# A wait between groups of gathers, and another order of the steps of tile 1

## The reference, cut to what matters

```python
def _L0_rec_ref(dense_features, sparse_features):
    combined = jnp.concatenate([dense_features[:, None, :], sparse_features], axis=1)
    interactions = jnp.einsum('bfd,bgd->bfg', combined, combined)
    iu, ju = jnp.triu_indices(FEATURE_NUM, k=1)
    return interactions[:, iu, ju]
e = jnp.stack([tbl_0[ids[:, 0]], ..., tbl_25[ids[:, 25]]], axis=1)
z = _L0_rec_ref(r_dense_features, e)
h = jnp.concatenate([z, r_dense_features], axis=1)
h = jnp.maximum(h @ W_top1 + b_top1, 0.0)
h = jnp.maximum(h @ W_top2 + b_top2, 0.0)
y = h @ W_top3
```

## Time and profile before

| | us |
|---|---|
| time, median of 3 runs | 511.42 (511.13 to 512.32) |
| the profiled execution's own time | 512.17 |
| its span, first to last instruction | 510.4 |
| TensorE busy | 360.0 (71%) |
| GpSimd busy | 254.2 (50%), 256 gathers |
| VectorE busy | 242.9 (48%) |
| ScalarE busy | 153.6 (30%) |
| mean granted clock of TensorE | 0.839 of full speed |

### The profile page before, as it was taken

One profiled execution on the slowest core, in us unless ns is written; L12 is line 12 of the kernel. 1 busy time (PEld: TensorE's weight loads), 2 busy tenths in 40 slices (PEclk: granted clock), 3 DMA queues, 4 the chain that ended last, 5 costly groups with the idle time before them and its releaser, 6 DMA issues.

```text
span 510.4 us, 13987 instructions
## 1 busy us (share of the span) xinstructions
PE 360.0 (71%) x6224; PEld 332.2 (65%) x6224; DVE 242.9 (48%) x172; ACT 153.6 (30%) x269; POOL 254.2 (50%) x260
## 2 busy tenths in 40 slices
PE   7695516977279763989369782897459882798927
PEld 6583406966179762989259781896439881797826
DVE  4995703827048270745429370673509451380220
ACT  2462401234122331324132241233232341223512
POOL 5887560655506474265635755264734745165000
PEclk9988656999569995899759986898959986698978
DMA  7992230211202131121303112131312112111000
GB/s 198 251 278 54 55 90 7 79 43 51 78 17 80 36 87 46 34 65 39 94 26 77 46 45 79 29 74 31 102 31 66 47 41 84 26 54 41 16 15 1
DMA packets 23322, 33.32 MB, mean 65 GB/s; under 512 B 6565, under 2 KB 15397, under 8 KB 23303
## 3 DMA queue, kind: packets, MB, share of 16 engines
q0 software_dynamic: 8192, 16.79, 12.6%
q1 hardware_dynamic: 14926, 16.20, 11.8%
q10 hardware_dynamic: 186, 0.09, 0.1%
HBM read 29.97 MB, written 0.01 MB: 59 GB/s over the span
## 4 chain that ended last, share of the span: by engine, by line
PE 56%; issue 18%; another core or an unknown queue 14%; ACT 7%; DMA 3%; SPq 2%; DVE 1%; ACTq 0%; DVEq 0%
PE psum L458 31%; PE psum L483 11%; PE psum L472 3%; DMA lows<-table 3%; ACT feats L336 3%; PE psum L548 3%; PE psum L496 2%; PE psum L497 2%; PE psum L498 2%; ACT gram L336 2%; PE psum L540 1%; ACT h L378 1%; SPq L208 1%; ACT dense_hi L336 1%
## 5 line engine op out<-in xcount | busy, mean ns | idle before, releaser
L252 POOL DMA_INDIRECT rows<-table,idx x256 | 254.0, 992 | 215.0 <-PE psum L472 114.2
L277 DVE TENSOR_TENSOR onehot<-ids_b,psum 125x2048 fp32r<-125x2048 int16 x80 | 180.2, 2283 | 18.5 <-PE psum L458 12.3
L260 DVE COPY gram<-psum 26x416 f32<-26x416 f32 x64 | 37.4, 584 | 182.6 <-PE psum L483 181.1
L336 ACT ACTIVATE feats<-psum 128x512 f32<-128x512 f32 (+1 forms) x120 | 77.4, 689 | 148.1 <-PE psum L458 106.9
L458 PE MATMUL psum<-onehot,hot_hi 125*128 125x256 f32 x640 | 99.2, 299 | 11.1 <-issue 6.8
L483 PE MATMUL psum<-feats 128*26 128x26 f32 x4096 | 64.3, 211 | 59.6 <-issue 55.7
L483 PEld LDWEIGHTS psum<-feats 128*26 128x26 f32 x4096 | 55.9, 125 | 70.8 <-issue 64.8
L458 PE MATMUL psum<-onehot,hot_lo 125*128 125x256 f32 x640 | 95.6, 291 | 4.4 <-issue 4.3
L458 PEld LDWEIGHTS psum<-onehot,hot_hi 125*128 125x128 f32 x640 | 86.5, 200 | 14.2 <-issue 9.0
L458 PEld LDWEIGHTS psum<-onehot,hot_lo 125*128 125x128 f32 x640 | 86.7, 198 | 6.3 <-issue 5.6
L336 ACT ACTIVATE gram<-psum 26x416 f32<-26x416 f32 (+1 forms) x72 | 35.5, 494 | 73.1 <-PE psum L483 54.5
(11 more groups left out here) (26 smaller groups left out, 167.7 us busy)
## 6 DMA issues: line engine op xcount, KB each, us to landing
lows<-table SPq DMA_DIRECT2D x10, 448.0 KB
rows<-table,idx POOLq DMA_INDIRECT x256, 2.5
ids_b<-hot_ids SPq DMA_DIRECT2D x8, 384.0 KB
ids_b<-hot_ids SPq DMA_DIRECT2D x8, 256.0 KB
rows<-dense SPq DMA_DIRECT2D x16, 64.0 KB
lows<-w SPq DMA_DIRECT2D x1, 1024.0 KB
pairs<-gram SPq DMA_DIRECT2D x16, 39.0 KB
lows<-table SPq DMA_DIRECT2D x10, 52.0 KB
```

The lines of the kernel that those rows point to most:

```text
L252: pool.indirect_dma_start(out=rows[:, f, :], out_offset=None, in_=tables[f - 1], in_offset=bass.IndirectOffsetOnAxis(ap=idx[:, 2 * s + t, ...
L260: return nc.vector.tensor_copy(o, x)
L277: nc.vector.tensor_tensor(onehot[f % SLOTS][0:HP_ROWS, :, :], ids_b[0:HP_ROWS, f:f + 1, :].to_broadcast([HP_ROWS, HC, SB]), psum[0:HP_ROWS ...
L336: return nc.scalar.activation(o, x, ACT.Copy)
```

## The change

Two things are changed. GpSimd waits before each group, besides for the free place in `rows`, until the group in front of it has landed (`wait_landed`): for group g > 0 the group g-1 of the same tile, for group 0 the last group of the tile before. The very first group waits for neither. And in `STEPS`, rows 1-2 comes ahead of the dense rounding, rows 1-3 and 1-4 ahead of layer 2, and gram 1 ahead of layer 3. No computation and no DMA is added or removed.

```diff
     STEPS = (TILE0[:7] + [("round_pairs",)] + TILE0[7:] + [("layer", "1a"), ("gram", 0)] + TILE1[:1]
-             + [("layer", "1b")] + TILE1[1:2] + [("dense",)] + TILE1[2:3] + [("layer", "2")] + TILE1[3:]
-             + [("layer", "3"), ("gram", 1)])
+             + [("layer", "1b")] + TILE1[1:3] + [("dense",)] + TILE1[3:] + [("layer", "2"), ("gram", 1), ("layer", "3")])
...
         @block.gpsimd
         def _(pool):
+            def wait_landed(s, t, g):
+
+                if g > 0:
+                    t0, g0, s0 = t, g - 1, s
+                else:
+                    t0, g0, s0 = 1 - t, NG - 1, s - (t == 0)
+                if s0 >= 0:
+                    pool.wait_ge(gathered[t0][g0], 16 * sum(f > 0 for f in GROUPS[g0]) * (s0 + 1))
+
             pool.wait_ge(idx_in, 16)
             for s in range(TURNS):
                 for t in range(2):
                     for g, features in enumerate(GROUPS):
                         wait_rows_free(pool, s, t, g)
+                        wait_landed(s, t, g)
```

## The result

The changed kernel takes 551.98 us (median of 4, 550.75 to 554.68) against 511.87 us for the one before: 1.0792 times, interval 1.0749 to 1.0836. I had forecast 501 us. The profiled execution took 554.68 us, its span is 552.9 us.

What follows compares the result with a forecast made beforehand. It took TensorE, held back by long gather trains, as today's bound and GpSimd's gather chain as the next: 74 + 7 x 55.9 - 0.3 = 465.0 us, gram 1 ends at 474.4, span 499.8, time 501 us; range 484 to 510.

Steps and rivals of the forecast that it cites:

- 2.77 us from issue to issue: GpSimd between groups: 2.5 us of landing plus 0.27 us of restart, ten times a turn.
- GpSimd's chain becomes the bound: Middle turns: GpSimd's gathers and awaited landings take 55.9 us, above TensorE's path of about 48 us.
- GpSimd's restart after a released wait costs 0.27 us: At each group's first gather: 0.27 us from the wait's release to the gather's start, ten times a turn.
- rival B: Each wait costs more, by a 0.5 us restart or 3 us landings: 58.3 us a turn, 518 us; chance 0.07.
- I add 0.7 us: Each turn of GpSimd's chain: 0.7 us for last gathers landing late beside SyncE's transfers, 55.2 to 55.9 us.
- The first turn: Beside the tables' load, 8 us taken per landing: turn 2's first gather at 74 us, against 55.68 before.
- In fours: With at most 4 gathers in a row, TensorE's signals are 0 to 3 us late; its path about 48 us.
- GpSimd doesn't wait for transposes: At tile 1's group 0, GpSimd arrives after tile 0's first transposes end, with 15 us of slack.
- The last turn: After the last landing: transpose 0.25, layer 2 3.62, gram 1 2.56, low clock 3 us; the rest stays.
- The low clock: Last turn's layer 2 and gram 1: TensorE runs slower after idling, 3 us added.
- The fixed cost by the Trainium skill: Landing of a 64 KB gather: 2.15 us estimated, taking 24 us off the time; the forecast used 2.5 us.
- C: Any gathers delay TensorE's signals; layer 2 and grams stay late: 60 us a turn, 529 us; chance 0.07.

Runs made afterwards that it cites:

- e2: The waits for landings alone, in the old order of steps, against the kernel before (510.56 us): 551.94 us, 1.0796 times.
- g2: The changed kernel, unchanged, run again in a set where the kernel before takes 383.67 us: 546.0 us, 1.4186 times.
- g3: The changed kernel with its two waits swapped, landing first, in a set where the kernel before takes 383.67 us: 515.85 us.
- e1: The new order of steps alone, without the waits for landings, against the kernel before (510.56 us): 512.71 us, 1.0047 times.
- e3: The changed kernel with its two waits swapped, landing first, where the kernel before takes 510.56 us: 522.84 us, 1.0247 times.
- k3: The changed kernel with waits swapped, landing first, each group awaiting the group two in front: 392.88 us against 385.02 before, 1.021 times.

## Why the prediction was wrong, step by step

The step that failed is the price of a landing that GpSimd waits for: 2.77 us from issue to issue, ten times a turn, with 0.7 us a turn for late ones. The runs showed 3.53 us.

**GpSimd's chain becomes the bound: right.** e2 shows that the new order costs nothing behind the waits, g2 that the time falls by 1% only when TensorE is relieved of the hold.

**"GpSimd's restart after a released wait costs 0.27 us": the term that failed most.** I read it from a gather that carries its only wait. The change gives all ten groups of a turn a second wait, and the one that ends last stands in an instruction ahead. Measured: 0.76 us behind the landing, in the median of 70 places. The difference, 10 x 0.49, is 4.9 us a turn by this (4.7 between g2 and g3), some 33 us over seven turns; swapping the two waits took 29 us off the time with the hold and 30 without. No row of the trace before has a gather with two waits, and so the term needed bounds, which I didn't give it: rival B's 0.5 us of restart was the only place where it could be larger, and it had 0.07 together with another cause.

**"I add 0.7 us" for landings that come late: too small.** Median steps are what I reckoned (2.81 and 2.78 in the swapped kernel), but the mean lies 0.22 to 0.27 us above, 2.2 to 2.7 us a turn. Less the 0.7 us allowed for, that is 10 to 14 us over seven turns. The row had the maximum beside the median, 4.4 against 2.5; a chain pays the mean of ten, not the median.

**The first turn: right in kind, 5 us short.** 79.05 against 74. Tile 0's groups came out as forecast (next tile's first gather at 48.23 against 47.4). Tile 1 took 30.8 us against 27.6, of which 5 x 0.49 = 2.5 us is the same restart; one us I had rounded away. The 8 us for a landing beside the tables' load were a choice between two far rows; the two groups priced at 12 us took 13.8 and 9.1, so this is right in the sum and not in each.

**"In fours" TensorE's path becomes short, 48 us: half right.** The signals are on time: layer 2's relu starts as its matmuls end.

```profile
337.03 0.84 ACT L387 ACTIVATE h<-psum,b_sb 128x256 f32<-128x256 f32 x2 [1.93 <-PE psum L549]
```

The grams aren't helped. TensorE in gram 1 of the same turn (start, length, records, idle ahead):

```profile
333.35 3.64 PE L549 MATMUL psum<-h,w_sb 128*128 128x256 f32 x16
336.92 0.53 PE L492 MATMUL psum<-feats 128*26 128x26 f32 x41
337.77 0.26 PE L492 MATMUL psum<-feats 128*26 128x26 f32 x5 [0.32 <-issue]
338.52 0.25 PE L492 MATMUL psum<-feats 128*26 128x26 f32 x4 [0.49 <-issue]
...
342.09 1.53 PE L492 MATMUL psum<-feats 128*26 128x26 f32 x110 [0.51 <-issue]
343.86 0.31 PE L492 MATMUL psum<-feats 128*26 128x26 f32 x5 [0.23 <-issue]
...
348.95 0.86 PE L492 MATMUL psum<-feats 128*26 128x26 f32 x53 [0.51 <-issue]
```

While a group of four is in flight, five or so matmuls come every 0.7 us; in the pause between two groups 110 come at once. The gram takes 12.9 us, and gram 0 of the same turn 13.1; they are among the longest, the others from turn 2 on take 7.7 to 13.2, but for the last. Over all 16 grams, busy time and the idle time ahead make 10.1 us each ((78.8 + 82.2) / 16), where the page before made 7.7 ((64.3 + 59.6) / 16). Both parts of the change do this under the hold: e1, the order alone, has 11.0 us and e2, the waits alone, 9.7. In e3 this path shows: the gather of 341.06 waits 5 us for a transpose, and that turn takes 61.5 us by first gathers (308.65 to 370.14). From 195 us on TensorE waits for no landing in e3, and from there to the last landing, at 486.05, a turn takes 58.2 us in the mean; g3, without the hold, has TensorE waiting 11 to 14 us a turn for landings, and 57.7 us. So my estimate of TensorE's path under the hold is near 58 us a turn, and a GpSimd chain of 55.9 us would have gained little; no run has that chain and the hold. My 48 us took the hot part as proof for fours. But the hot part doesn't show the hold: its units follow each other every 4.25 us in the changed kernel with the hold (transposes at 293.01, 297.26 and 301.51) and without (278.79, 283.06, 287.31). The gram does. Why is argued only: the hot part's matmuls have 256 columns and take some 0.12 us each, the gram has 256 records of about 0.01 us, so a pause between issues shows there first. The earlier trace rows had shown it for grams and I read it as a matter of long trains.

**GpSimd doesn't wait for transposes: right for the changed kernel**, where the last transposes' signal and the landing come together (79.05 is such a row, its landing's wait is what sets it). In the swapped kernel, which is faster, it does in four of the 70 places.

**The last turn: right.** 33.4 us from the last landing to the end, 34.8 forecast. The low clock came too: after 3.3 us of idle time layer 2 takes 6.32 us there at a granted clock of 0.56, near the low level, against 3.62 at 1.00 in the kernel before, near the 3 us added. e2, with layer 2 ahead of the last landing, gains nothing that shows.

**The fixed cost by the Trainium skill.** The landings stayed at 2.5 to 2.6 us in the median in all sets, so the 2.15 us estimated from the Trainium skill, DMA: Bandwidth & Descriptors, section Anatomy of one DMA, didn't come true for these gathers. The advice of the Trainium skill, same page, section Rules for kernel authors, to issue early and wait late, is what k3 against g3 shows in numbers: 392.9 against 515.9 us for the same waits one group later.

**The rivals.** B had the mechanism, waits that cost more, but its 518 us has 17 of the 51 us that were missing. C's premise was half true under the hold: the grams stay long, layer 2's signal does not stay late, and neither is what set the time, as g2 takes 546.0 us without the hold. That C's 529 us was the nearest number is luck. The sign was wrong because the forecast had 2.4 us a turn between the new bound and the old turn, and two terms of its chain, each multiplied by ten, were too small: one stood at a row with a single wait, the other near the median.

## What to carry to other kernels

Before you add a wait to an instruction that already has one, see which of the two ends last and let the instruction carry that one: here the order in which two waits were written was worth 29 us of 552. A wait for the landing of what was just issued costs 1.8 us (swapped) to 2.3 us over the usual step each time, 3.0 and 3.5 against 1.25; the wait for the group before that cost 8 us in all, 5.7 of them in the first turn. Where a chain of equal steps becomes the bound, price the step by its mean, late ones included, and give each term that is multiplied by ten its own bounds.

## What the hardware showed that I had not expected

The kernel before takes 511 us in one condition and 384 us in another, with the same gathers, the same 1.25 us step and the same 2.5 us landing. What differs, of all that was compared, is TensorE's issue and its signals beside gathers in flight (a gram of 24.5 us against 7.5). The changed kernel takes 552 and 546 us in the two. So its worth is 1.08 or 1.42 times the time before, and 1.08 tells more of the hold than of the change. What brings the hold about, and whether moving gathers off the grams pays under it, no run here shows.
